# Three edits to a one-core transformer layer: where block 3's queries and keys lie, one unread TensorE product, and the order of the second feed-forward layer

## The reference, cut to what matters

```python
x = x + 0.5 * ffn(layernorm(x))          # 128 -> 512, exact gelu, 512 -> 128
x = x + attention(layernorm(x))
x = x + 0.5 * ffn(layernorm(x))
# attention: key j is open to query i if j % 4 == 0 or abs(i - j) <= 8
scores = jnp.einsum('bhqd,bhkd->bhqk', q, k) / sqrt(D)
attn = softmax(where(allowed, scores, -inf))
out = einsum('bhqk,bhkd->bhqd', attn, v) @ o_w + o_b
# ffn: h = butterfly(x @ W_exp + b_exp, up); h = gelu(h + up_bias)
#      y = butterfly(h, down) @ W_con + b_con + down_bias
```

## Time and profile before

| | us |
|---|---|
| median of three runs | 271.96 |
| the profiled execution, its own time | 274.41 |
| its span, first to last instruction | 272.3 |
| mean granted TensorE clock | 0.994 of full |
| PE busy | 252.1 (93%) |
| ACT busy | 196.4 (72%) |
| DVE busy | 126.7 (47%) |

### The profile page before, as it was taken

How to read it: one execution, slowest core, us unless ns; L and a number is a source line. 1 busy time by engine, 2 the same in 40 slices (tenths; PEclk the granted TensorE clock), 3 DMA queues, 4 the chain that set the end, 5 groups by cost and what they waited for, 6 DMA issues and landing times.

```text
span 272.3 us, 6938 instructions
## 1 busy us (share of the span) xinstructions
PE 252.1 (93%) x2919; PEld 139.2 (51%) x2919; DVE 126.7 (47%) x408; ACT 196.4 (72%) x256; POOL 7.3 (3%) x12
## 2 busy tenths in 40 slices
PE   2697899999797999999999999999999999899995
PEld 0482765858442444355444445444454444486655
DVE  4868358897676232134354236224325520555311
ACT  1854155586667999998899988999978999634430
POOL 9100000000000000000000000000000000000000
PEclk9999999999799999999999999999999999999999
DMA  6940000287769723311311330332130000001111
GB/s 205 259 114 12 2 1 0 87 234 197 162 144 360 243 82 84 82 43 46 87 50 34 84 84 2 85 82 59 27 84 2 4 0 2 2 0 41 39 39 39
DMA packets 23887, 21.82 MB, mean 80 GB/s; under 512 B 4743, under 2 KB 22087, under 8 KB 23835
## 3 DMA queue, kind: packets, MB, share of 16 engines
q1 hardware_dynamic: 22742, 21.02, 28.8%
q10 hardware_dynamic: 1112, 0.34, 0.6%
HBM read 13.98 MB, written 7.56 MB: 79 GB/s over the span
## 4 chain that ended last, share of the span: by engine, by line
PE 84%; DVE 8%; ACT 5%; issue 1%; DMA 1%; ACTq 0%; DVEq 0%
PE ps L662 22%; PE ps L640 21%; PE ps L488 11%; PE ps L447 9%; PE ps L647 4%; PE ps L672 3%; PE ps L461 2%; PE ps L680 2%; PE ps L511 2%; PE ps L692 1%; PE ps L473 1%; ACT gelu_h L758 1%; PE ps L524 1%; DMA resid<-L_attn_x 1%; PE ps L512 1%
## 5 line engine op out<-in xcount | busy, mean ns | idle before, releaser
L860 ACT ACTIVATE probs_all<-ps 128x1024 f32<-128x1024 f32 x128 | 122.8, 1023 | 12.8 <-PE ps L640 9.4
L662 PE MATMUL ps<-probs_all,v_strided 128*32 128x256 f32 x1024 | 68.2, 384 | 1.5 <-ACT probs_all L860 1.5
L640 PE MATMUL ps<-q_slots,k_strided 75*128 75x512 bf16 x250 | 65.2, 381 | 0.3 <-ACT probs_all L860 0.3
L662 PEld LDWEIGHTS ps<-probs_all,v_strided 128*32 128x32 f32 x1024 | 27.2, 109 | 33.1 <-issue 9.5
L1136 DVE RECIPROCAL rden<-ps 128x16 f32<-128x16 f32 x16 | 4.1, 258 | 72.1 <-PE ps L680 72.1
L640 PEld LDWEIGHTS ps<-q_slots,k_strided 75*128 75x128 bf16 x250 | 20.4, 97 | 33.6 <-issue 9.8
L758 ACT ACTIVATE gelu_h<-ps,bias_up 128x512 f32<-128x512 f32 x32 | 21.9, 687 | 21.3 <-PE ps L447 21.2
L488 PE MATMUL ps<-down_folded,gelu_h 128*128 128x128 f32 x256 | 30.5, 277 | 2.7 <-ACT gelu_h L758 2.7
L488 PEld LDWEIGHTS ps<-down_folded,gelu_h 128*128 128x128 f32 x256 | 29.2, 192 | 5.2 <-ACT gelu_h L758 3.3
L447 PE MATMUL ps<-xnorm_t,up_folded 128*128 128x512 f32 x64 | 29.3, 600 | 1.7 <-ACT xnorm_t L749 1.0
L1162 DVE SCALAR_TENSOR_TENSOR probs_all<-probs_all,mask_k_sb 128x1024 f32<-128x1024 f32 x16 | 19.6, 1223 | 4.5 <-ACT probs_all L864 4.0
(11 more groups left out here) (116 smaller groups left out, 210.5 us busy)
## 6 DMA issues: line engine op xcount, KB each, us to landing
q_slots<-q_parts SPq DMA_DIRECT2D x16, 288.0 KB
k_local<-k_local_parts SPq DMA_DIRECT2D x48, 78.0 KB
q_parts<-prologue_or_parts SPq DMA_DIRECT2D x9, 384.0 KB, 4.6
k_strided<-k_strided_parts SPq DMA_DIRECT2D x12, 96.0 KB
q_parts<-last_parts SPq DMA_DIRECT2D x3, 384.0 KB, 4.8
k_local_parts<-prologue_or_parts SPq DMA_DIRECT2D x3, 288.0 KB, 5.1
resid<-L_attn_x SPq DMA_DIRECT2D x1, 768.0 KB, 10.2
out<-resid SPq DMA_DIRECT2D x3, 256.0 KB, 2.3
```

The lines of the kernel that those rows point to most:

```text
L640: mm = pe.matmul(PS[:, b0 + i, :], KS[:, ch, G * g + h, :], QS[:, g, h, :], start=True, stop=True)
L662: mm = pe.matmul(PS[VC * h:VC * (h + 1), 6 + n % 2, 0:QB // 2], VS[:, ch, at:at + VC], probs, start=(ch == 0 and r == 0), stop=False, skip ...
L860: act.activation(PE_[:, ch // 2, 2 * m:2 * m + 2, ch % 2, :], PS[:, b0:b0 + 2, :], ACT.Exp).then_inc(p_ready, 1)
```

## The change

Block 1's and block 3's queries and keys (`QK[1]`) move from stretches 14 and 15 to 18 and 19, behind the probabilities. The sixth exponential then waits for the splits of block 2 alone, and the ninth, which overwrites `QKR`, waits for the last one. PE gets one unread product (two passes) into bank 0 ahead of block 3's `turn_rows`, and one less between the first scores. In the second FFN `ffn_down` comes one `ffn_up` later; the odd blocks' gelu goes to a second buffer in stretches 0 to 3 of `ARENA` (`hidden`), `ffn_down` of the last block waits for bank 5 only ahead of its third tile, and DVE normalizes one block further ahead.

```diff
-        QK = [ARENA[:, o:o + 2 * QB] for o in (12 * QB, 14 * QB)]
+        QK = [ARENA[:, o:o + 2 * QB] for o in (12 * QB, 18 * QB)]
...
+        def hidden(b):
+            return GH if b % 2 == 0 or b < NB else ARENA[:, 0:NC * QB].rearrange("p (c q) -> p c q", c=NC)
+
...
                 pe.wait_ge(g_ready, NC * (b + 1))
-                if b % NB:
+                last = b % NB == NB - 1
+                if b % NB and not last:
                     pe.wait_ge(y_done, b)
                 for t in range(TB):
+                    if last and t == 2:
+                        pe.wait_ge(y_done, b)
                     for c in range(NC):
-                        mm = pe.matmul(down_bank(b, t)[:, t * P:(t + 1) * P], GH[:, c, t * P:(t + 1) * P], DNW[:, c, :],
+                        mm = pe.matmul(down_bank(b, t)[:, t * P:(t + 1) * P], hidden(b)[:, c, t * P:(t + 1) * P], DNW[:, c, :],
                                        start=(c == 0), stop=(c == NC - 1))
...
                     norm_sums(NB - 2)
+                    pe.wait_ge(y_first, 1)
+                    keep_clock(0, 1)
                 if b:
                     turn_rows(b - 1)
...
-            keep_clock(4, 2)
+            keep_clock(4, 1)
             first_score(2, 0).then_inc(first_read, 1)
...
-            for b in range(NB, 2 * NB):
-                if b > NB:
-                    ffn_up(b)
+            transpose_block(NB + 1)
+            project(NB - 1)
+            for b in range(NB + 1, 2 * NB):
+                ffn_up(b)
                 if b < 2 * NB - 1:
                     transpose_block(b + 1)
-                if b == NB:
-                    project(NB - 1)
-                ffn_down(b)
+                ffn_down(b - 1)
+            ffn_down(2 * NB - 1)
...
                     if b and c == 0:
-                        act.wait_ge(y_ps, b)
+                        act.wait_ge(y_ps, b if b <= NB else b - 1)
...
-                    act.activation(GH[:, c, :], PS[:, 1 + c, :], ACT.Gelu, bias=BUP[:, c:c + 1]).then_inc(g_ready, 1)
+                    act.activation(hidden(b)[:, c, :], PS[:, 1 + c, :], ACT.Gelu, bias=BUP[:, c:c + 1]).then_inc(g_ready, 1)
...
                             if u == 0 and s == 5:
-                                act.wait_ge(split, split_seen(NB - 1, 2))
+                                act.wait_ge(split, split_seen(NB - 2, 2))
                                 act.wait_ge(sq_done, NB + 2)
...
                             if u:
                                 act.wait_ge(o_ps, u)
+                            else:
+                                act.wait_ge(split, split_seen(NB - 1, 2))
...
             finish_unit(NB - 1, NG - 1)
+            ffn_ahead(NB + 1)
             finish_block(NB - 1)
             dve.wait_ge(x2_done, NB)
             layernorm((NB - 1) * TB, TB)
-            ffn_sum(NB)
-            for b in range(NB + 1, 2 * NB):
-                if b < 2 * NB - 1:
-                    ffn_ahead(b)
+            ffn_ahead(NB + 2)
+            for b in range(NB, 2 * NB):
                 ffn_sum(b)
```

## The result

The changed kernel takes **269.77 us** (median of four runs, 269.30 to 270.01) against 272.20 us before (four runs, 271.92 to 272.75): ratio **0.9906, 95% interval 0.9884 to 0.9929**, 2.4 us less. The sum said 4.15 us and 267.8 us; the range ended at 269.2. Direction right, size wrong.

What follows compares the result with a forecast made beforehand. PE, busy 93% of the span, was taken as the bound, so only removing its pauses or starting stretches earlier helps. 1.3 + 0.85 + 2.0 = 4.15 us off 271.96 gave 267.8 us, range 266.8 to 269.2.

Steps and rivals of the forecast that it cites:

- The sum: Whole kernel: 1.3 + 0.85 + 2.0 = 4.15 us off the 271.96 us median, giving 267.8 us.
- the 0.68 us by the flag: Block 3's queries and norm sums: with the clock kept at 2.4 GHz, the flag comes 0.68 us earlier.
- gain of 0.85 us: ACT's first exponential starts 0.85 us earlier: 0.68 by the flag, 0.17 by the product removed between the first scores.
- the 2.45: Median of the runs shown lies 2.45 us below the profiled time; the same 4.15 us was taken off it.
- The rivals: Clock falls anyway at the old place, 269.0 us, chance 0.18; one slow stretch at the branch, 269.5 us, chance 0.04.
- The sixth exponential's wait, 1.3 us: First attention unit: the sixth exponential no longer waits for DVE's last split, so PE's values start 1.3 us earlier.
- The price of the unread product: Ahead of block 3's transposes: two added PE passes, 0.86 us, partly hidden, start the keys' product 0.58 us later.
- What it brings: After block 3's transposes: the clock stays at 2.4 GHz, so the norm sums come at 74.74 instead of 75.42.
- The branch as the next limit: Between the first scores: one product fewer gains only 0.17 us, as PE then waits about 0.6 us at the branch.
- The second FFN, 2.0 us: Second FFN: the new order removes PE's pauses for gelu ahead of down products, 0.51 us twice and 0.95 once.

Runs made afterwards that it cites:

- the move alone: Kernel before with only the odd blocks' queries and keys address and the two exponential waits changed; ratio 0.9972 (0.9923 to 1.0021).
- the faster group on the other chip: Unchanged kernel before, timed beside the changed kernel's repeat and three variants; seven runs from 271.81 to 272.81 us, mean 272.43.

## Why the prediction was wrong

The step that failed is the last sentence of the sum: "the same 4.15 off 271.96". The terms were worked out against one profiled execution, and one of them, the 0.68 us by the flag, exists only in an execution whose clock falls. The profiled one was of that kind; the runs whose median I took it off were not. With a start of 10.77 instead of 12.10 us, the two edits of unread products together are no gain of 0.85 us but a loss of 11.20 - 10.77 = 0.43. By that the sum is 1.3 - 0.4 + 2.0 = 2.9 us, 269.1, inside the range. The signs were there: 274.41 us lies 2 us above the highest timed run, and I named the 2.45 and carried it through as a constant. The rivals asked whether the clock would fall in the changed kernel; none asked whether it falls in the runs of before.

Term by term:

- *The sixth exponential's wait, 1.3 us.* Right: 1.2 in the trace of the move alone, 1.0 and 1.1 between groups of times. It does not depend on the clock. Nothing took its place; DVE's last split was in time.
- *The price of the unread product.* Right: the keys' product starts 71.44 - 67.67 = 3.77 behind the mark instead of 71.18 - 68.02 = 3.16, 0.6 later where 0.58 was said.
- *What it brings.* Right against an execution with the half clock: norm sums 6.68 behind the mark instead of 7.40, 0.72 where 0.68 was said. Right too that the clock then stays up: the granted clock is 0.999 or 1.00 in all 29 executions of the five kernels with that product, and 0.993 or 0.994 in 18 of 51 without it. Wrong in how often there is anything to bring.
- *The branch as the next limit, 0.17 us for the product removed.* Right: 0.19, and PE waits 0.51 us in the row where about 0.6 was said. The branch has 497 ns in the row again, not the 108 that the Trainium skill gives (Advanced Engine Details and Errata, Control Flow Timing), and the start is not 0.4 us earlier as by that figure. A slip in the prediction: it says that by 108 ns the fifth product would be the limit. By its own numbers that product starts at 79.48 - 0.68 - 0.86 = 77.94 and the sixth could follow at 78.16, while the branch would end at 78.3; the branch would still be last.
- *The second FFN, 2.0 us.* Slightly low. The rest is 270.4 - 85.43 = 184.97 in the single execution of before with the full clock and 267.5 - 84.80 = 182.70 in the changed kernel: 2.27 us, by the times 2.1. The three down products that had a pause in front of them are also shorter without it (3.74 against 3.84 us).

Against an execution of before with the half clock the forecast was close: from the mark to the end of the span it is 272.3 - 68.02 = 204.28 and 267.5 - 67.67 = 199.83, 4.45 us for 4.15. Against the single execution with the full clock it is 270.4 - 67.41 = 202.99, so 3.16 us. The times say 2.4 in the first comparison, with an interval of about 1.9 to 3.2, and 269.54 against 272.43, 2.9, against the faster group on the other chip. Some of what is missing to 3.16 may be that the faster executions of before are those with a short start of the program (last section), which the changed kernel has only in part. The early group there has a mean of 5.78 us in the four full-clock traces without the product and 6.14 in the six with it; an estimate from that takes 0.35 us off the 3.16 and leaves 2.8. It rests on few traces: argued, not shown.

## What to carry to other kernels

Before a trace is priced, its own execution must be held against the timed runs. If it lies outside them, some term in it is not typical, and a granted clock below 1.00 in one stretch is the first to suspect: such a term is a chance, not a constant. An unread product that holds the clock up is an insurance: here its premium is 0.4 to 0.6 us, and it saves 1.3 us, before the premium, about one time in three, so the mean time hardly moves and only the spread shrinks. Put into a pause of PE its premium nearly goes in the trace (start 10.70 and 10.59 us against 10.57 without it); the times do not show that. And the distance between two groups of times is not the cost of what tells them apart: 0.76 of 2.1 us lay elsewhere.

Removing cover work in front of a branch gains only until the branch itself is late: the sequencer's rows of that line give the limit.

## What the runs showed of the hardware

In the traces without the product ahead of the transposes, what happens at about 17 us goes with whether the clock falls at 71 us. Early in the program PE makes 32 passes of 128 columns (L461; L464 in the changed kernel), as many as in a down product, which takes 3.74 us at full clock. Timeline of PE in the single execution of before whose clock stayed up:

```profile
11.40 5.78 PE L461 MATMUL ps<-probs_all 128*128 128x128 f32 x32 [0.79 <-ACT probs_all L820]
```

and in the one whose clock fell:

```profile
11.39 6.52 PE L461 MATMUL ps<-probs_all 128*128 128x128 f32 x32 [0.79 <-ACT probs_all L820]
```

In the four traces with the half clock at 71 us this group took 6.38, 6.50, 6.52 and 6.65 us; in the four without it and without the product ahead of the transposes 5.62, 5.67, 5.78 and 6.06. The pace changes once inside the group. Windows of the execution whose clock stayed up, then of the other:

```profile
16.20:16.80 0.60, 0.60 (x8) 0.60 (x8) 0.43 (x1) 0.17 (x1) 0.00 (x0) 1.00 0.21 58
```

```profile
16.20:16.80 0.60, 0.60 (x5) 0.60 (x4) 0.42 (x1) 0.17 (x1) 0.00 (x0) 1.00 0.29 39
```

Up to 15.60 both have about 5 passes of PE in such a window; the first reaches 7 in the next one (8 behind it), the second 8 only in the window from 17.40. So what moves against the program from one execution to the next seems to be early or late at both places; the link is read from eight traces and tested by none. The Trainium skill, TensorE: Matmul & The Clock Gate, Part 1, says that the moments at which the clock changes are not tied to the kernel's start and vary between runs; these eight traces agree. What sets it in a given execution stays open. The granted clock in the windows reads 1.00 during these early groups as well, so it cannot be taken at its word there.

By this sign five of the six traces with the product prove little of what it does, since their group took 5.79 to 6.26 us, below every one that fell. The sixth, with the product behind the transposes, lies among those that fell and yet has clock 1.00 throughout:

```profile
11.40 6.58 PE L464 MATMUL ps<-probs_all 128*128 128x128 f32 x32 [0.78 <-ACT probs_all L829]
```

The stronger evidence for the product is the count of executions above, none of 29 against 18 of 51.
